# One PSUM ring of seven banks, and hand tables for the order of the middle batches, in a gated cross-attention and experts kernel

## The reference, cut to what matters

```
n  = layernorm(x)                                    # 512 x 256
q, k, v    = n @ Wq + bq, n @ Wk + bk, n @ Wv + bv   # 16 heads of 16 channels
qc, kc, vc = n @ Wcq + bcq, ctx @ Wck + bck, ctx @ Wcv + bcv     # ctx: 1601 x 128
y  = softmax(mask(q k^T / 4)) v + softmax(qc kc^T / 4) vc        # causal self part + cross part
x1 = x + tanh(g0) * (y @ Wp + bp)
n2 = layernorm(x1)
route  = top 4 of softmax(n2 @ Wg) over 32 experts, with a capacity for each
x2 = x1 + tanh(g1) * (sum over the 4 of weight * swiglu_e(n2) + swiglu_shared(n2))
```

## Time and profile before

| | |
|---|---|
| time, median of 3 runs | 4762.45 us (4757.96 to 4764.63) |
| the profiled execution, its span | 4808.0 us |
| fourteen middle batches in that span | 338.7 to 3796.2 us, 3457.5 us |
| PE busy | 4323.8 us (90%) |
| DVE busy | 3532.5 us (73%) |
| ACT busy | 2688.0 us (56%) |
| POOL busy | 1651.4 us (34%) |

### The profile page before, as it was taken

The page is one execution under the profiler, slowest core; times in us unless marked ns, Lnnn a source line. Parts: engine busy times, 40 slices in busy tenths (PEclk is TensorE's granted clock), DMA queues, the critical chain, the costliest instruction groups (busy, mean ns, idle before and its releaser), DMA issues. The chain is left out here.

```text
span 4808.0 us, 75133 instructions
## 1 busy us (share of the span) xinstructions
PE 4323.8 (90%) x25317; PEld 1906.7 (40%) x25317; DVE 3532.5 (73%) x7733; ACT 2688.0 (56%) x5523; POOL 1651.4 (34%) x2163
## 2 busy tenths in 40 slices
PE   5999999999999999999999999999999995688882
PEld 2333333334343433333333333333333332577771
DVE  5788788888878787878788878788888783344443
ACT  1665656565656565665656565656665653344440
POOL 1122323232323232323232232323232314488883
PEclk7999999999999999999999999999999997899996
DMA  5443545454444344545444545454544444888888
GB/s 118 71 91 75 109 84 106 81 111 81 106 81 104 73 104 84 110 84 108 86 104 87 102 82 107 80 104 90 100 94 99 95 97 131 184 150 150 151 150 245
DMA packets 363501, 513.23 MB, mean 107 GB/s; under 512 B 64124, under 2 KB 227820, under 8 KB 363176
## 3 DMA queue, kind: packets, MB, share of 16 engines
q1 hardware_dynamic: 268240, 380.43, 38.0%
q0 software_dynamic: 87728, 115.39, 13.6%
q10 hardware_dynamic: 7208, 13.26, 0.9%
HBM read 288.49 MB, written 201.27 MB: 102 GB/s over the span
## 5 line engine op out<-in xcount | busy, mean ns | idle before, releaser
L688 ACT ACTIVATE prob<-scores 128x512 f32<-128x512 f32 (+3 forms) x4352 | 2141.6, 561 | 1268.5 <-PE scores L492 1251.6
L882 DVE TENSOR_REDUCE pmx<-ring 128x1 f32<-128x512 f32 (+1 forms) x3328 | 1999.1, 664 | 165.1 <-PE ring L570 158.3
L492 PE MATMUL scores<-stacks 98*128 98x512 bf16 (+3 forms) x4352 | 1291.0, 370 | 79.5 <-ACT prob L688 31.0
L514 PE MATMUL outs<-prob,vt 128*32 128x512 f32 x8704 | 1094.3, 575 | 4.9 <-POOL prob L1084 3.9
L570 PE MATMUL ring<-stacks 96*128 96x512 bf16 x3072 | 971.4, 389 | 64.1 <-DVE pmx L882 55.6
L492 PEld LDWEIGHTS scores<-stacks 98*128 98x128 bf16 (+1 forms) x4352 | 341.0, 99 | 1299.4 <-ACT prob L688 736.3
L1598 POOL DMA_INDIRECT scratch_sums<-e_yo,e_tok x320 | 496.3, 1551 | 116.7 <-issue 84.1
L882 DVE TENSOR_REDUCE mc<-ring 128x1 f32<-128x128 f32 (+3 forms) x1024 | 437.3, 483 | 123.1 <-PE ring L587 119.0
L1084 POOL TENSOR_SCALAR_AFFINE_SELECT prob<-prob 128x512 f32<-128x512 f32 x256 | 168.4, 658 | 1045.9 <-ACT prob L688 1036.0
L1154 POOL TENSOR_TENSOR split<-rest,split 128x512 bf16<-128x512 f32 (+1 forms) x224 | 218.8, 977 | 803.5 <-DVE split L976 803.0
L570 PEld LDWEIGHTS ring<-stacks 96*128 96x128 bf16 x3072 | 301.2, 99 | 450.9 <-DVE pmx L882 184.6
(11 more groups left out here) (165 smaller groups left out, 3751.4 us busy)
## 6 DMA issues: line engine op xcount, KB each, us to landing
stacks<-scratch_parts SPq DMA_DIRECT2D x768, 128.0 KB, 7.2
stacks<-scratch_parts SPq DMA_DIRECT2D x384, 136.1 KB, 10.0
scratch_parts<-split SPq DMA_DIRECT2D x64, 768.0 KB, 4.5
e_xin<-scratch_slots SPq DMA_DIRECT2D x160, 289.0 KB
scratch_parts<-split SPq DMA_DIRECT2D x32, 816.8 KB, 4.5
num<-oc POOLq DMA_DIRECT2D x256, 64.0 KB
den<-scratch_inverses POOLq DMA_DIRECT2D x63, 256.0 KB, 8.4
ct<-in_ctx_t_dram SPq DMA_DIRECT2D x16, 800.5 KB, 8.1
```

The source lines that it names most:

```text
L492: eng.matmul(ps[0:m, k, q0:T], kst[g][0:KR + 2, j, k0:k0 + m], qst[g][0:KR + 2, j, qc + q0:qc + T], start=True, stop=True).then_inc(scored ...
L514: mm = eng.matmul(po[32 * j:32 * j + 32, q0:T], vt[ch][0:m, VW * vi + VE * hl:VW * vi + VE * hl + 32], prob[0:m, n % 2, j, q0:T], start=kt ...
L688: eng.activation(prob[0:m, n % 2, j, q0:T], ps[0:m, i % SB, q0:T], ACT.Exp, scale=SCALE).then_inc(exped.sem, 1)
L882: eng.tensor_reduce(dst, src, AX.X, ALU.max).then_inc(free_of(part, it), 1)
```

## The change

1. **One ring.** `scores` and `ring` become one tensor of seven banks. Every tile, score or item, takes the next bank in the order in which PE issues them. `claim` waits for whatever stood in that bank seven tiles before: the exponential, if it was a score, or the reader's `freed` event, if it was an item's tile. `earlier_score` finds the last user in the part before. This holds for all kinds of batch.
2. **Weighted sums from a table.** `SUMS_AT` says for each slot of a middle batch where the weighted sum of the slot before goes: 0, right behind pair 0; 1, behind the items of pair 0; 2, right behind pair 1; 3, at the end, as before. It has 7 zeros, 14 ones, 20 twos and 27 threes. The other kinds keep 3.
3. **Places from tables.** In middle batches `PLACED` gives the half slot of every other item, and the new `MAXIMA` (one table for the batch) the number of maxima in each half slot. The places of F and L shift by one here and there.
4. **Order in a half slot.** `DEFERRED` becomes `WHOLE_ARRAY`, with `trans`, `router` and `rank` added. They go last in a half slot, and first in one whose weighted sum stands between the scores and the items.

The same instructions run on every engine; none is added or removed. The diff, with the tables cut:

```diff
-RB, SB = 4, 3
+RB = 7
...
-DEFERRED = ("split", "value", "shift", "outproj", "hidden", "shared")
+WHOLE_ARRAY = ("trans", "split", "value", "shift", "outproj", "router", "hidden", "shared", "rank")
...
+PLACED = {
...
+    "finish_a": (8, 24, 29, 29, 30, 31, 37, 40, 42, 42),
...
+}
+MAXIMA = (
+    5, 0, 3, 3, 6, 2, 0, 3, 3, 1, 0, 4, 5, 2, 3, 2, 1, 4, 2, 4, 0, 2, 3, 1, 1, 4, 0, 4, 5, 1, 1, 1, 0, 0,
...
+SUMS_AT = (
+    1, 2, 1, 3, 2, 3, 3, 3, 3, 2, 0, 2, 3, 3, 1, 3, 1, 3, 1, 3, 1, 1, 2, 3, 3, 3, 2, 2, 2, 3, 3, 3, 3, 2,
...
-    return [sorted(here, key=lambda it: it[0] in DEFERRED) for here in out]
+    first = {2 * n + p // 2 for n in range(SLOTS) for p in (0, 2) if sums_at(kind, n) == p}
+    return [sorted(here, key=lambda it: (it[0] in WHOLE_ARRAY) != (n in first)) for n, here in enumerate(out)]
...
+        def claim(what):
+            nonlocal n
+            k = n % RB
+            self.bank[what], self.turn[what], self.before[what] = k, self.uses[k], self.last[k]
+            n += 1
+            return k
...
-        ps = ctx.enter_context(nc.psum_tensor("scores", [128, SB, 512], F32))
         pm = ctx.enter_context(nc.psum_tensor("ring", [128, RB, 512], F32))
...
+            def claim(part, what, turn):
+
+                k, before = PLANS[part.kind].bank[what], PLANS[part.kind].before[what]
+                if before is None:
+                    score = earlier_score(part.kind, k)
+                    if score is not None:
+                        pe.wait_ge(exped, part, score + 1)
+                elif before != "ring":
+                    pe.wait_ge(exped, part, before + 1)
+                    return pm[:, k, :]
+                pe.wait_ge(freed[k], part, turn)
+                return pm[:, k, :]
...
-                    k = i % SB
-                    before = i - SB if i >= SB else max(j for j in range(4 * SLOTS) if j % SB == k) - 4 * SLOTS
-                    pe.wait_ge(exped, part, before + 1)
+                    dst = claim(part, i, PLANS[part.kind].turn[i])
...
+                    at = sums_at(part.kind, n) if n or not part.first else None
                     for pair in range(2):
                         scores(part, n, pair)
+                        if at == 2 * pair:
+                            weighted(part, n - 1)
                         for it in items[2 * n + pair]:
                             item(part, it)
-                    if n or not part.first:
-                        weighted(part, n - 1)
+                        if at == 2 * pair + 1:
+                            weighted(part, n - 1)
```

More of the change, by code:

```diff
@@ L170, in plan, with deal @@
     out, load = [[] for _ in range(2 * HALF)], [0.0] * (2 * HALF)
-    def deal(at, places, items, cost):
+    def deal(name, at, places, items, cost):
+        if kind == "M":
+            at, places = 0, PLACED[name]
         for n, it in zip(places, items, strict=True):
@@ L178, in fill @@
         if kind == "M":
-            for n, k in zip(range(lo, hi), MAXIMA[lo]):
-                out[n] += items[:k]
-                items = items[k:]
+            for n in range(lo, hi):
+                out[n] += items[:MAXIMA[n]]
+                items = items[MAXIMA[n]:]
             assert not items
@@ L237, in __init__, with earlier_score @@
         self.bank, self.turn, self.number, self.uses = {}, {}, {}, [0] * RB
-        n = 0
-        for here in self.items:
+        self.before, self.last = {}, [None] * RB
+        n = entries = 0
+        def claim(what):
[4 more added lines that the diff above has]
+            return k
+        for h, here in enumerate(self.items):
+            if kind in "FML":
+                for i in (2 * h, 2 * h + 1):
+                    self.last[claim(i)] = i
             for it in here:
                 for i in range(BANKS.get(it[0], 0)):
-                    self.bank[it, i], self.turn[it, i], self.number[it, i] = n % RB, self.uses[n % RB] + 1, n + 1
-                    self.uses[n % RB] += 1
-                    n += 1
-        self.entries = n
+                    k = claim((it, i))
+                    entries += 1
+                    self.uses[k] += 1
+                    self.turn[it, i], self.number[it, i], self.last[k] = self.uses[k], entries, "ring"
+        self.entries = entries
 PLANS = {kind: Plan(kind) for kind in PARTS}
+def earlier_score(kind, k):
+    last = [PLANS[was].last[k] for was in {"P": "", "F": "", "M": "FM", "L": "M", "X": "L"}[kind]]
+    last = [i for i in last if i is not None and i != "ring"]
+    return max(last) - 4 * SLOTS if last else None
 def build_attention(nc, B, x, ctx_t, w, scr, stacks, wall, table):
@@ L687, in exps @@
                     act.wait_ge(summed, part, n - 1)
-                    eng.activation(prob[0:m, n % 2, j, q0:T], ps[0:m, i % SB, q0:T], ACT.Exp, scale=SCALE).then_inc(exped.sem, 1)
+                    eng.activation(prob[0:m, n % 2, j, q0:T], pm[0:m, PLANS[part.kind].bank[i], q0:T], ACT.Exp, scale=SCALE).then_inc(exped.sem, 1)
             def outs(part, n):
@@ L884, in item @@
                     g = it[1]
-                    for last in max_items(g)[0][-RB:]:
-                        read(dve, part, last)
+                    newest = {bank_of(part, it, i): (it, i) for it in max_items(g)[0] for i in range(BANKS[it[0]])}
+                    for last, i in newest.values():
+                        read(dve, part, last, i)
                     eng.tensor_reduce(mc[g % 2][:, :].rearrange("p (h a q) -> p h a q", a=2, q=NQ)[:, :, 0, :], pmx[:, :, :, :],
```

58 lines of the change are left out of this document (37 added, 21 removed), and 7 rows, old and new, of the table MAXIMA.

## The result

The changed kernel takes 4786.38 us (median of four runs, 4784.25 to 4787.68) against 4760.2 (4756.99 to 4764.63) for the kernel before on the same chip: ratio 1.0053, interval 1.0039 to 1.0067. It is slower by 0.5%. The forecast was 4697 us, with a range up to 4780; the result lies outside it, on the side that had the smaller chance.

A forecast was written before the change was run, and what follows sets the result against it. The bound changes between PE and DVE by stretch, and spare time is lost. Balance -3.6, added waits +2.0 and ring -3.1 give -4.7 us a batch, times 14 = -66 us: 4697 us, range 4610 to 4780.

The forecast's parts named there:

- what lies outside the fourteen batches: Batches F, L, P and X take the ring but little else: 0 us change, within 5 us.
- the ring: Scores in middle batches wait less with seven shared banks: 3.1 us a batch saved, bounds 0 and 11.0.
- Slots 14 to 19: Loses 10 cross maxima, a rest and a transpose; PE's idle 1.7 us goes: 22.3 becomes 17.9, -4.4 us a batch.
- I cost the moves at nothing: New places of the 68 weighted sums between scores and items in a batch: 0, with up to 2 us of waiting.
- Slots 20 to 29: Gains 2.7 us of PE work and a 1.8 us projection, PE still setting the pace: +4.5 us a batch.
- the direct dependencies: Three pairs now adjacent on PE in slots 20 to 29, each waiting about 1.0 us: +2.0 a batch, bounds 0 and 3.
- Slots 30 to 37: Gains 9 cross maxima, loses a projection, becomes DVE's stretch at 92% busy: 31.0 us, +2.3 a batch.
- Slots 38 to 47: Loses 9 cross maxima, DVE falls to 29.4 us, at 92% busy 31.9: -6.0 us a batch.
- The bursts: Rival: half slots of five or more tiles stall the common ring, +8.0 us a batch, 4873 us; chance 0.12.
- The clock rival: Rival: more half slots with scores alone lower PE's clock, +6.1 us, net +1.4 a batch, 4782 us; chance 0.10.
- the ratio 0.9905: Median of the plain runs over the profiled span, used to turn the forecast span 4742 into 4697 us.
- three signs of being wrong: Slots 20 to 29 grow much over 7 us, scores wait for DVE over 5 us a batch, or batches' clock below 0.98.

The follow-up runs named there:

- before_again: The kernel before, with no edit, run once more for a second profile: 4751.0 us, span 4749.2.
- sums_end: after_newton_late with every weighted sum put back at the end of its slot: 4746.46 us, ratio 0.9908.
- spaced: after_newton_late with the router, the first shared and the first projection one half slot later: 4654.64 us, ratio 0.9717.
- spaced_alone: The changed kernel, POOL's steps unmoved, with the router, first shared and first projection one half slot later: 4752.33 us, ratio 0.9923.
- tables_only: The changed kernel's order with banks as before, three for scores and four for items: 4948.58 us, ratio 1.0394.
- ring_only: Seven banks in one ring, with the places, maxima, order and end-of-slot weighted sums of the kernel before: 4756.71 us, ratio 0.9981.
- after_newton_late: The changed kernel with POOL's sixteen inverse-root steps moved behind the mask of slot 16: 4687.03 us, ratio 0.9849.

## Why the prediction was wrong

Measured against before_again, a middle batch grew from 243.1 to 246.3 us, and what lies outside the fourteen batches shrank by 10 us, where the forecast had 0 within 5. The plain runs differ by 26 us. Measured less forecast, the four stretches below are off by +5.4, +1.7, -2.5 and +0.6 us a batch, the 3.1 booked for the ring appear in none, and the other stretches gave -0.3: in all 8.0, which is the distance from -4.7 to +3.2.

- **Slots 14 to 19, forecast -4.4, measured +1.0. This is the step that failed.** It says: "DVE falls from 20.0 to 13.5 us, so PE's idle 1.7 us of slots 16 and 17 goes too". DVE did fall (14.6). But slots 16 and 17 had a second engine in line, POOL, and the earlier trace rows show it: busy 3.77 of 7.90 us with 17 instructions. The prediction read that row for DVE and PE and never asked what POOL did. With fewer maxima PE came to its weighted sum early and stood 4.55 us for POOL's mask, and its clock fell behind the wait. With POOL's chain behind the mask the stretch takes 16.6 us, 1.3 less than the 17.9 forecast. So the counts and unit costs were near, and one queue was missing. These 5.4 us a batch are 76 of the 89 us between forecast and result. The place of that weighted sum, the end of slot 17, is the same before and after. "I cost the moves at nothing" was off too, but the other way: the places gain 2.0 to 3.6 us a batch (sums_end).
- **Slots 20 to 29, forecast +4.5 for the load and +2.0 for the direct dependencies, measured +8.2.** The load came out as forecast: 47.8 forecast, 47.9 in spaced. The dependencies were found at their places, with waits of 0.94, 0.77 and 0.76 us, near the 1.0 forecast. Their sum, 2.5 a batch, is between the 2.0 taken and the 3.0 of all three. What was missing is the fall of the clock behind the first of them, 1.1 us a batch. POOL's wait has no part in this stretch: it takes 47.9 us in spaced_alone too.
- **Slots 30 to 37, forecast +2.3, measured -0.2.** DVE was busy 27.3 of 28.5 us, 96%, not the 28.7 reckoned, and PE waited for it only 0.2 us a batch. The 92% were taken from slots 38 to 47, where DVE's steps are held by POOL's products; that this made them a poor guide was not tested.
- **Slots 38 to 47, forecast -6.0, measured -5.4, in the repaired kernels -5.7 to -6.1.** Right. What still holds this stretch is the scores' wait for DVE, 34.0 us in fourteen batches.
- **The ring, forecast -3.1, bounds 0 and -11.** This term was mis-sized. Alone it gives 0.2%, some 9 us and not 43. Of the 70.4 us of scores' idle time in the earlier trace rows from which it was taken, 26.4 (1.9 a batch) are for ACT; 26.6 are "issue", for which the profile shows nothing that was waited for. The second profile of before has no such wait of 3 us or more in sum, so this was nothing that a bank could save. In the new order it carries the tables (tables_only). The scores' wait for ACT fell from 20.9 us in before_again to 4.1, but that for DVE came in its place.
- **Rivals.** The bursts did not stall the ring. The clock rival gave a time near the result, 4782, but for another reason. Its size was fair: with 195 us at the lower clock against 72, at most half of the 123 more is lost, 62 us or 4.4 a batch by an estimate from the second table, near its 6.1. The Trainium skill (TensorE: Matmul & The Clock Gate, A second HAM failure mode: psum-queue depth-cycling) tells of a kernel that cycles through PSUM banks, in which the matrix engine stands idle for short times between groups of matmuls and the clock goes down and up. Here the same seven banks are cycled in spaced with 44 us at the lower clock, fewer than the 72 of before_again, in the changed kernel with 195, and in ring_only with 157. So the cycling does not decide. The idle times do, and in this the trace agrees: in the changed kernel the clock falls behind distinct waits of PE, of 4.55 us in slot 17 (all fourteen batches), 0.77 in slot 21 (twelve) and up to 2.9 ahead of slot 43 (all), and removing the first two removed their falls, each alone (after_newton_late, spaced_alone). The half slots with scores alone stay in these kernels, so they did not make the first two falls; whether they have a part in the one of slot 43, which stands among them, is open.
- **The base.** The forecast rested on a span of 4808.0 us, 48 above the plain runs. Taking it by the ratio 0.9905 was harmless. With POOL's chain moved, the ratio 0.9849 is near the 0.9867 of the forecast, in part by luck: its errors in the ring (+3.1 us a batch), slots 20 to 29 (+1.7), 30 to 37 (-2.5) and 14 to 19 (-1.3) largely cancel. The repaired order (spaced) is 2.8% faster than before.
- **The signs.** Of the three signs of being wrong, the granted clock came (0.97 in the fourteen batches, below 0.98), slots 20 to 29 grew by 8.2 us against the 7 named, and the scores' wait for DVE stayed at 2.4 us a batch, under its 5.

What stays open: why slots 51, 55 and 56 take 3 us more in some executions than in others; where the weighted sums' 1.0% comes from beyond the scores' shorter wait for DVE; and the wait for DVE in slots 42 and 43, which no edit removed without a larger loss.

## What to carry to other kernels

When work is taken out of a stretch that one engine bounds, list every engine's queue there, the idle ones too, and ask of each when it delivers what PE needs; here a chain of sixteen tiny instructions ahead of one that PE waits for cost their number by 0.28 us as soon as its cover went. Keep two items apart of which one reads the other's copy; half a slot was enough here. Price a wait on PE with what follows it: the 4.5 us wait here cost 7.0, and the waits of 2.5 us a batch cost 3.6.

## What the runs showed of the hardware

DVE instructions of some kinds that begin while a POOL product runs are held until it ends: steps of 0.29 us took 2.07 and up to 2.5, and a 128x16 step of 0.165 took a mean of 2.13. One that began just before the product was not held (L1014, 0.18 us). Reductions were not held: L974 began 0.11 us into a product and took 0.29, and its longest over 64 is 0.288 us. In the changed kernel 30 of the routing's steps with two tensor inputs (L975, L976, L982, L983) began inside one of POOL's two products, and all took 1.0 to 2.5 us; of 81 reductions that did (L974, L981, and 70 of L940, which reads PSUM) none took longer than elsewhere. The Trainium skill (SBUF — State Buffer, Who interferes with whom) says that a DVE instruction with two SBUF inputs contends with a POOL instruction that reads SBUF, that the contention is an exclusive lock, that issue order decides who blocks, and that a reduction never contends. The trace agrees: L975 began behind the product and was held, L1014 began ahead of it and was not, L974 was never held. L1013 has one tensor input, and was held all the same; the page says that tensor_scalar can run in a mode that contends with POOL, and no run here tells whether it did.
